# A two-layer graph kernel: front and edge steps re-ordered, a sum moved from POOL to PE, the bias added a step later

## The reference

```python
h = jnp.maximum(_layernorm(x, axis=-1), 0.0)
x = x + L0(h, adj)      # attention over the edges
h = jnp.maximum(_layernorm(x, axis=-1), 0.0)
x = x + L1(h, adj)      # hyperbolic midpoint over the edges

# L0
node_att = jax.nn.softmax(x @ node_w, axis=0)
h = x @ edge_w
e = jnp.where(adj > 0, h @ h.T, NEG_BIG)
edge_att = jax.nn.softmax(e, axis=1)
output = adj * (node_att * edge_att) @ (x @ weight) + bias

# L1: XW = mobius_matvec(W, X); gamma from the row lengths of XW
two_mean = (A @ (gamma * XW)) / clamp_abs(A @ (gamma - 1.0))
...         # two_mean scaled row by row, tanh and artanh of row lengths, relu
```

## Time and profile before

| | us |
|---|---|
| median of 3 runs (lowest, highest) | 722.23 (719.67, 728.56) |
| profiled execution | 725.74 |
| its span, first to last instruction | 724.0 |
| busy PE, DVE, POOL, ACT | 495.6, 471.4, 396.6, 350.2 |
| front, edge steps, second layer, last stage | 0 to 90, to 457, to 513, to 724 |

### The profile page before, as it was taken

One profiled execution on the slowest core, in us unless ns is written; L12 is line 12 of the kernel. 1 busy time (PEld: TensorE's weight loads), 2 busy tenths in 40 slices (PEclk: granted clock), 3 DMA queues, 4 the chain that ended last, 5 costly groups with the idle time before them and its releaser, 6 DMA issues.

```text
span 724.0 us, 12785 instructions
## 1 busy us (share of the span) xinstructions
PE 495.6 (68%) x3804; PEld 413.5 (57%) x3804; DVE 471.4 (65%) x1977; ACT 350.2 (48%) x718; POOL 396.6 (55%) x458
## 2 busy tenths in 40 slices
PE   3588463949698596988867877895266674757660
PEld 2367342738587485977766766784155553545440
DVE  3476757886877578686878578685444254476744
ACT  3596663655573555647340556477121121244553
POOL 4043537375655663566566610066477777777740
PEclk9798865959989899898989999998599798998885
DMA  8954579887879657786532400004433333335621
GB/s 310 394 204 173 189 283 366 291 314 254 291 232 369 219 219 266 244 342 211 185 94 67 101 17 1 1 1 148 147 97 99 103 100 97 97 106 159 193 75 59
DMA packets 38161, 128.92 MB, mean 178 GB/s; under 512 B 6224, under 2 KB 23504, under 8 KB 34000
## 3 DMA queue, kind: packets, MB, share of 16 engines
q1 hardware_dynamic: 22736, 84.87, 31.2%
q0 software_dynamic: 15360, 43.29, 21.3%
HBM read 115.49 MB, written 12.65 MB: 177 GB/s over the span
## 4 chain that ended last, share of the span: by engine, by line
PE 25%; DVE 25%; issue 13%; POOL 12%; ACT 9%; DMA 8%; DVEq 6%; ACTq 1%; POOLq 0%; SPq 0%
POOL work L1497 12%; PE bank L826 8%; DMA work<-in_adj 5%; PE bank L765 3%; ACT work L622 3%; DVE fs L1060 3%; PE bank L1589 2%; DVEq L1215 2%; PE bank L253 2%; PE bank L1768 2%; PE bank L797 2%; DMA table_h<-front 2%; DVE work L1104 1%; ACT L1211 1%; PE bank L810 1%
## 5 line engine op out<-in xcount | busy, mean ns | idle before, releaser
L720 POOL DMA_INDIRECT work<-table_h,work x160 | 161.4, 1009 | 99.6 <-issue 71.6
L1497 POOL DMA_INDIRECT work<-table_y,idx x128 | 130.7, 1021 | 39.0 <-issue 38.7
L622 ACT ACTIVATE work<-work 128x2048 bf16<-128x2048 f32 x64 | 121.6, 1902 | 45.6 <-DMA work<-in_adj 30.2
L826 PE MATMUL bank<-work 128*128 128x128 f32 x640 | 98.9, 318 | 15.7 <-DVEq L1106 15.7
L826 PEld LDWEIGHTS bank<-work 128*128 128x128 f32 x640 | 92.5, 230 | 17.5 <-DVEq L1106 15.0
L1589 PE MATMUL bank<-work 128*128 128x257 f32 x256 | 74.5, 442 | 19.8 <-DMA work<-table_y,idx 19.8
L765 PE MATMUL bank<-work 128*128 128x256 bf16 x512 | 70.8, 292 | 12.8 <-ACT work L622 12.8
L1589 PEld LDWEIGHTS bank<-work 128*128 128x128 f32 x256 | 55.4, 222 | 35.6 <-DMA work<-table_y,idx 26.4
L1585 PE MATMUL bank<-work 128*128 128x257 f32 x128 | 40.1, 440 | 48.9 <-ACT work L1600 40.5
L1362 DVE SCALAR_TENSOR_TENSOR fs<-work 128x256 f32<-128x256 f32 x32 | 13.7, 427 | 84.6 <-ACTq L1617 84.2
L765 PEld LDWEIGHTS bank<-work 128*128 128x128 bf16 x512 | 51.8, 104 | 27.3 <-ACT work L622 17.2
(11 more groups left out here) (271 smaller groups left out, 1006.6 us busy)
## 6 DMA issues: line engine op xcount, KB each, us to landing
work<-in_adj SPq DMA_DIRECT2D x32, 2048.0 KB, 9.7
table_y<-work SPq DMA_DIRECT2D x8, 520.0 KB, 3.7
gx<-in_x SPq DMA_DIRECT2D x8, 512.0 KB, 8.5
table_h<-front SPq DMA_DIRECT2D x8, 512.0 KB, 4.7
front<-in_x POOLq DMA_DIRECT2D x8, 512.0 KB, 5.0
out<-gx SPq DMA_DIRECT2D x8, 512.0 KB, 3.4
work<-table_h,work POOLq DMA_INDIRECT x160, 6.1
work<-table_y,idx POOLq DMA_INDIRECT x128, 2.8
```

The source lines that it names most:

```text
L622: a.activation(abf[:, u % HALVES, :], adu[:, b % 2, h, :], ACT.Copy, accum_out=cnt[:, k, b, h:h + 1]).then_inc(L["conv"], 1)
L720: p.indirect_dma_start(gat[:, k, n, :], None, table_h, bass.IndirectOffsetOnAxis(ix[:, k, n:n + 1], 0)) \
L826: last = t.matmul(bank[4 + b % 2][:, c * P:(c + 1) * P], gat[:, k, n, c * P:(c + 1) * P], otp[:, n, :], start=(q == 0), stop=(q == TILES - 1))
L1497: p.indirect_dma_start(gtm[:, n % OCT, q, :], None, table_y, bass.IndirectOffsetOnAxis(idx[:, n * TILES + q:n * TILES + q + 1], 0)) \
```

## The change

- SP: the sixth load of x and the store of group 0 come ahead of the second adjacency block, the weights and the bias behind all loads; blocks 2 to 5 are asked for after the stores of groups 1, 2, 4 and 6 (before: 1, 3, 5, 7).
- Front, beside the steps: units 3 to 7 are converted a step sooner and packed with them, `keys` run in steps 5 and 8 (before 6 and 9), the first list in step 9 (before 10), and four units of group 1 are converted in steps 9 and 10 (before two).
- Edge steps: ACT converts units 4 to 7 of group n and 0 to 3 of group n+1 (before 2 to 7 and 0, 1).
- Node softmax: the negation behind `edges`, the exponential behind the conversions, the sum over the partitions by a matmul with a matrix of ones, a step later.
- Bias: POOL adds it a step after the load, behind the next group's gathers.
- `spill_counts` in step 8, `spill_totals` amid POOL's gathers of step 8, `spill_places` in step 9, all 32 `spill_moves` on POOL behind the last aggregation.

```diff
+        STORED = (1, 2, 4, 6)
+        CONV_AT = (1, 2, 3, 3, 4, 5, 6, 7)
+        PACK_AT = (2, 3, 4, 4, 6, 6, 7, 8)
...
         def early_act(a):
             def beside(n):
-                if 1 <= n <= UNITS * GB:
-                    unit_conv(a, 0, 0, n - 1)
+                for u in range(UNITS * GB):
+                    if n == CONV_AT[u]:
+                        unit_conv(a, 0, 0, u)
+                if n == NG + 1:
+                    unit_conv(a, 1, 1, 0)
                 if n == NG + 2:
-                    unit_conv(a, 1, 1, 0)
-                    unit_conv(a, 1, 1, 1)
+                    for u in range(1, HALVES):
+                        unit_conv(a, 1, 1, u)
...
-                if ls and not at_:
-
-                    a.wait_ge(s_negmax, 1)
-                    a.activation(natt[:, :], logit[:, :], ACT.Exp, bias=cs(1)[:, 1:2], accum_out=cs(0)[:, 2:3])
-                    a.drain().then_inc(s_exp, 1)
...
-                for u in range(2, UNITS * GB):
+                for u in range(HALVES, UNITS * GB):
                     conv(u, wd)
+                conv(0, ahead)
+                conv(1, ahead)
+                if ls and not at_:
+                    a.wait_ge(s_negmax, 1)
+                    a.activation(natt[:, :], logit[:, :], ACT.Exp, bias=cs(1)[:, 1:2], accum_out=cs(0)[:, 2:3])
+                    a.drain().then_inc(s_exp, 1)
                 for b in (2, 3):
                     aggregate(b)
...
-                conv(0, ahead)
-                conv(1, ahead)
+                conv(2, ahead)
+                conv(3, ahead)
...
                         if n == GT // 2:
                             p.wait_ge(L["agg"], GB * g + GB)
                             p.sem_inc(s_go, 1)
+                            if isinstance(g, int) and g == NG - 1:
+                                spill_totals(p)
...
                     p.wait_ge(L["x1"], GB * g + GB)
-                    p.dma_start(xr2[:, k, :, :], x_r[:, grp(g), :]).then_inc(L["x"], 16)
-                    p.wait_ge(L["x"], 16 * (g + 1))
+                    p.dma_start(xr2[:, k, :, :], x_r[:, grp(g), :]).then_inc(L["x"][k], 16)
+                if at_:
+                    g, k = at_
+                    p.wait_ge(L["x"][k], 8 * (g - k) + 16)
                     for b in range(GB):
                         p.tensor_tensor(xr2[:, k, b, :], xr2[:, k, b, :], bias_bc[:, :], ALU.add)
                     p.drain().then_inc(L["xb"], 1)
...
                 exp_g(0, GT // 4)
+                if at_ and not ag_:
+                    t.wait_ge(s_exp, 1)
+                    t.matmul(exp_sum, ones, cs(0)[:, 2:3], start=True, stop=True).then_inc(s_sum, 1)
                 pack(2)
                 pack(3)
...
-                if n == 6:
+                if n == 5:
                     keys(d, 0, 0, 0, (6, 7))
+                if n == NG:
+                    keys(d, 0, 0, 1, (6, 7))
                 if n == NG + 1:
-                    keys(d, 0, 0, 1, (6, 7))
+                    edge_list(d, 0, 0, None)
                 if n == NG + 2:
                     d.drain()
                     d.tensor_reduce(cs(0)[:, 0:1], logit[:, :], AX, ALU.max)
                     d.drain().then_inc(s_red, 1)
-                    edge_list(d, 0, 0, None)
...
                 if ls:
                     edges(*ls)
-                if at_ and not ag_:
-                    d.wait_ge(s_all, 2)
-                    d.reciprocal(cs(1)[:, 3:4], cs(1)[:, 2:3])
...
+                if ls and not at_:
+                    d.wait_ge(s_all, 1)
+                    d.tensor_scalar(cs(1)[:, 1:2], cs(1)[:, 0:1], -1.0, None, ALU.mult)
+                    d.drain().then_inc(s_negmax, 1)
                 n = ag_[0] + 3 if ag_ and isinstance(ag_[0], int) else 0
+                if n == NG:
+                    spill_counts(d)
+                if n == NG + 1:
+                    spill_places(d)
...
-            norm_scale(d, f, 2)
-            if sparse:
-                spill_places(d)
...
-            if sparse:
-                spill_moves(d, range(0, 8))
...
             load(4)
+            load(5)
...
+            store(0, 0)
+            load_block(e, 1, 1)
+            load(6)
+            load(7)
             e.dma_start(w0[:, :, :], weight.rearrange("(c p) d -> p c d", p=P)).then_inc(s_w2, 16)
...
-            for g in range(NG):
+            for g in range(1, NG):
                 store(g, g % 2)
-                if g % 2:
-                    load_block(e, g // 2 + 2, g // 2 % 2)
+                if g in STORED:
+                    n = STORED.index(g) + 2
+                    load_block(e, n, n % 2)
...
-            p.wait_ge(s_exp, 1)
-            p.partition_all_reduce(cs(1)[:, 2:3], cs(0)[:, 2:3], P, RADD)
...
             fast_pool(p)
-            spill_totals(p)
             fast_flag(p)
             p.wait_ge(X["places"], 1)
-            spill_moves(p, range(16, NB))
-            p.drain().then_inc(X["move_pool"], 1)
+            p.wait_ge(L["agg"], GB * NG + 2 * GB)
+            spill_moves(p, range(NB))
+            p.drain().then_inc(X["move"], 1)
             table_pool(p, bf)
```

More of the change, by code:

```diff
@@ L581, in gnn_program @@
         L["adj"] = [sem(f"fa_adj{n}") for n in range(2)]
+        L["x"] = [sem(f"fa_xr{k}") for k in range(2)]
         L["gat"] = [[sem(f"fa_gat{k}{b}") for b in range(GB)] for k in range(2)]
@@ L773, in beside @@
             def beside(n):
-                if 2 <= n <= UNITS * GB + 1:
-                    unit_pack(t, 0, n - 2, (6, 7))
+                for u in range(UNITS * GB):
+                    if n == PACK_AT[u]:
+                        unit_pack(t, 0, u, (6, 7))
             return beside
@@ L1116, in body @@
                 if ls and not at_:
-                    d.wait_ge(s_all, 1)
-                    d.tensor_scalar(cs(1)[:, 1:2], cs(1)[:, 0:1], -1.0, None, ALU.mult)
-                    d.drain().then_inc(s_negmax, 1)
-                if ls and not at_:
                     for k in (0, 1):
@@ L1150, in body @@
                     dots(*at_, GT // 4, GT // 2)
+                if at_ and not ag_:
+                    d.wait_ge(s_sum, 1)
+                    d.reciprocal(cs(1)[:, 3:4], exp_sum)
+                    d.drain()
+                    d.tensor_scalar(natt[:, :], natt[:, :], cs(1)[:, 3:4], None, ALU.mult)
+                if at_:
                     by_slot(*at_)
@@ L1376, in gnn_program @@
         idb2, o = arena(o, P, dt=BF16)
+        move, _ = arena(o, NB, SW, dt=BF16)
         mm2, o = arena(o, 2, CW, dt=BF16)
@@ L1390, in gnn_program @@
         spill_idx, o = arena(o, OCT)
-        move, o = arena(o, NB, SW, dt=BF16)
+        assert o <= SPILL_END, o
         assert o <= WORK, o
@@ L1407, in gnn_program @@
         F["spill"] = [sem(f"fm_spill{k}") for k in range(2)]
-        X = {n: sem("sx_" + n) for n in ("counts", "total", "places", "move_dve", "move_pool", "found", "idx")}
+        X = {n: sem("sx_" + n) for n in ("counts", "total", "places", "move", "found", "idx")}
         def spill_counts(d):
@@ L1445, in spill_places @@
             d.tensor_scalar(part[:, 1, :].bitcast(I32), fifth, KEY - 1, None, ALU.bitwise_and)
-            d.drain().then_inc(X["places"], 1)
+            d.drain()
             for v in range(2):
                 d.tensor_copy(parts[:, :, v], part[:, v, :].bitcast(I32))
+            d.drain().then_inc(X["places"], 1)
         def spill_moves(v, blocks):
@@ L1455, in spill_pe @@
         def spill_pe(t):
-            t.wait_ge(X["move_dve"], 1)
-            t.wait_ge(X["move_pool"], 1)
+            t.wait_ge(X["move"], 1)
             for o in range(NB // OCT):
@@ L1865, in _ @@
             e.dma_start(bias_bc[:, :], bias.rearrange("(a d) -> a d", a=1).broadcast_to([P, D])).then_inc(s_w2, 16)
-            for g in range(5, NG):
-                load(g)
-            load_block(e, 1, 1)
-            def store(g, k):
-                e.wait_ge(f0.h, GB * (g + 1))
-                e.dma_start(th_r[:, grp(g), :], hs[:, k, :, :]).then_inc(s_th[k], 16)
-            for g in range(NG):
+            for g in range(1, NG):
                 store(g, g % 2)
-                if g % 2:
-                    load_block(e, g // 2 + 2, g // 2 % 2)
+                if g in STORED:
+                    n = STORED.index(g) + 2
+                    load_block(e, n, n % 2)
             fast_load(e)
```

19 lines of the change are left out of this document (9 added, 10 removed).

## The result

The changed kernel takes 744.5 us (median of 4; 741.9 to 748.4) beside 724.8 for the kernel before (4; 719.7 to 728.6). The ratio is 1.029, 95% interval 1.024 to 1.034: slower, and outside the predicted range. The profiled execution took 748.42 us, its span is 746.7; it is 3.9 us above its median, and the profile before 3.5 us above the 722.23 of the first three runs.

What follows compares the result with a forecast made beforehand. No engine was taken to bound the whole; DVE bound steps 3 to 7. Terms -8.7 + 0.4 + 0 + 0.3 + 17.9 + 1.0 - 1.4 = +9.5 us gave 735.2 profiled, median 732, range 715 to 742.

Steps and rivals of the forecast that it cites:

- The mechanism that it named first: POOL's configuration pairs around the totals' all-reduce in step 8 delay new_x of step 9: +17.9 us; forecast's case, chance 0.50.
- I take **0** for 3 and 4: Steps 3 to 7: sooner conversions and the later bias add together cost nothing; bounds -2.2 and +5 us.
- the sum has 0.3: Step 8: spill_counts adds one DVE instruction and a drain, +0.3 us.
- Part 1: Front: reordered transfers, earlier keys and first list bring PE's first list matmul sooner, -8.7 us; bounds -3 and -14.
- Part 2: Node softmax's maximum and sum: nothing themselves; second list -0.6 more, start of step 2 slower, together +0.4 us.
- Part 3: Sooner conversions, steps 3 to 7: at most 2.2 us of DVE's packing waits could return; taken as 0.
- Part 4: POOL adds the bias a step later; new_x keeps 0.2 us slack, cost 0, upper bound +5 us over five steps.
- the third rival: Late bias bounds steps 4 to 8, 2.7 us longer each, 13 us in all, 745 us; chance 0.10.
- Part 5: Totals amid step 8's gathers: new_x of step 9 late by +17.9 us; bounds +4.8 and +19.
- The clock term: After PE's long stand in step 9 its granted clock falls: +1 us, range 0 to 4.
- +4.8 (no time for either pair): Totals in step 8: lower bound of their cost if both POOL pairs take no time, +4.8 us.
- Part 6: Places hidden in step 9, 32 matrices on POOL with 8.9 us to spare; first steps and second layer gain, -1.4 us.

Runs made afterwards that it cites:

- experiment 8: Kernel before with only the front's changes (load and store order, earlier conversions and packing, earlier keys and first list): 724.2 us beside 723.1, ratio 1.003.
- experiment 11: Changed kernel with the bias in its own step, totals by a PE matmul and ScalarE's conversions as before: 715.6 us, ratio 0.986 to the kernel before.
- experiment 9: Kernel before with the node softmax's changes alone, ratio 0.987, and with the front's changes too, 0.984, on a chip where the kernel before took 892.3 us.
- experiment 10: Changed kernel with the bias in its own step and totals by a PE matmul, run twice: 717.2 and 714.7 us, ratios 0.993 and 0.987 to the kernel before.
- experiment 5: Kernel before with the late bias alone, added behind the next group's gathers: 735.7 us beside 723.1, ratio 1.019.
- experiment 4: Changed kernel with the totals by a PE matmul instead of POOL's all-reduce, late bias kept: 729.1 us, ratio 1.011 to the kernel before.
- experiment 1: Changed kernel with the totals behind the last bias add and the places in step 10, late bias kept: 735.5 us, ratio 1.020 to the kernel before.
- experiment 2: Changed kernel with the bias added in its own step, totals still amid the gathers of step 8: 719.6 us, ratio 0.995 to the kernel before.
- experiment 6: Changed kernel with the bias add moved ahead of the next group's gathers, totals still amid step 8's gathers: 719.7 us, ratio 0.993 to the kernel before.
- experiment 3: Changed kernel with the bias in its own step, totals behind the last bias add and places in step 10: 721.4 us, ratio 0.998 to the kernel before.
- experiment 7: Changed kernel with one small POOL operation added in step 1: a copy, 744.9 us, ratio 1.031; then a tensor_tensor, 742.2 us, ratio 1.023 to the kernel before.

## Why the prediction was wrong

The forecast was 732 and its range ended at 742; it came to 744.5. The mechanism that it named first was there in full; what failed was the step "I take **0** for 3 and 4".

The profiled executions were to lie 9.5 us apart and lie 22.7 apart. Of the 13.2 us between, 8.8 came in steps 3 to 8, where the sum has 0.3 and the trace 9.1 (5.1, 1.2 and 2.8); there `new_x` waited 8.1 us for `xb`. The second list is 1.5 us behind its forecast, step 2 has 1.9 us more than it was given, step 9 has 2.0 more, the second layer 1.4 less, and the last stage 0.4 more.

*Part 1, the front.* -7.5 instead of -8.7, and L226 without a wait for the store. Right for the front, but not for what follows: alone it is worth nothing (experiment 8). Of the maximum and the exponential the text says that `edges` and the conversions no longer stand behind them, and it books that at nothing. It is this edit that moved the second list (experiment 11 against 8), and by experiment 9 perhaps without help from the front.

*Part 2.* The second list came at 112.6 (111.2 forecast). The all-reduce came at 95.8 instead of 91.7, as its pair took 9.8 us and not 6.3, and DVE's negation stood 3.4 us for it. Then step 2 lost 2.9 us where 1.0 stood: from the second list to its end 39.4 us, before 36.5. It is the conversions of group 2 ahead of the copies for PE, as the step had it, under-sized: with them as before (experiment 11) it is 36.4, with bias and totals alone undone (experiment 10) 39.5.

*Part 3, conversions,* 0, and measured the same (experiment 11): what they cost in step 2 comes back by the end, and no more.

*Part 4, the late bias.* Forecast 0, bounds -2.2 and +5; measured 12.6 us alone (experiment 5), 12.0 us with the totals on PE (729.1 against 717.2), and 25 us beside the totals on POOL (744.5 against 719.6). The drain of 4.61 us was the right row for the adds, and the releases in the loop came 5.1 to 5.5 us behind their start, half a microsecond more: `new_x` of steps 4, 6 and 7 waited 0.6 to 0.8 us for it, as the bound had it. What I left out is where the gathers end. I looked at the steady state, one step of 41.8 us, and there POOL is ahead. In steps 8 and 9 a step has no new group to find and is 34 us long, while POOL's twenty gathers and their wait for PE keep their length. There the adds start behind the last gather, at 412 to 414 in experiments 4 and 1, and `new_x` at 417 to 419.5 instead of 415. It could be read from the earlier trace rows: the load of x is issued at 413.36 for 0.80 us, and with 4.61 us for adds and drain the bias is there at 418.8, 3.8 us behind the 414.96. It is the mechanism of the third rival, for the most part in steps 8 and 9 rather than in each of steps 4 to 8; that rival's price, 13 us, is met by chance, and so is its 745 by the 744.5.

*Part 5, the totals.* Nearly exact, in part by luck. Of the shift of `new_x` in step 9, 414.96 to 437.33, 4.2 us were brought along from step 8; the other 18.2 stand against 17.9. The pairs took 5.7 and 7.8 us (6.3 and 8.0 forecast), the load of x is 7.3 us later by this part (6.5 forecast), and `new_x` starts 3.8 us behind the adds (4.6 forecast): the last two cancel. The clock term was 1 and is 2.7 us: from `new_x` to the end of step 9 it took 25.1 us, before 22.4, at a clock of 0.58 in the first ten. But "+4.8 (no time for either pair)" was wrong in kind. In size it is not what the part's own terms give, 17.9 - 6.3 - 8.0 = 3.6; without pairs, `new_x` measured from the end of step 8 came 4.3 us later (15.7 against 11.4), and all of that is the late bias. The totals cost 1 to 5 us while the bias is early (experiments 2 and 6 against 10) and 15 us while it is late (744.5 against 729.1): the second pair is on the way only if the adds come behind the all-reduce. The two parts are not a sum: each makes the other costlier, and I had put the whole of it on one of them.

*Part 6.* The places were hidden in step 9, as forecast; uncovered they cost some 5 us (24.2 against 19.3 us for step 10, experiment 3). The matrices took 29.69 us and were ready 7 us before POOL was wanted (8.9 forecast). The second layer, last `new_x` to the first gather of the last stage, went from 57.1 to 54.3 us, -2.8 instead of -1.4.

```profile
480.11 29.69 POOL L1480 TENSOR_SCALAR work<-work 128x256 bf16<-128x256 f16 x32 [33.00 <-PE bank L843]
509.97 0.20 POOL L1735 MEMSET work<- 128x128 f32 x1 [0.17 <-issue]
516.76 4.00 POOL L1724 TENSOR_SCALAR work<-work,col 128x256 f32<-128x256 f32 x4 [6.58 <-DVEq L1835]
```

The step of the first pair, 11.65 us ahead of the first add in step 2, has no term in the sum. Before the change it stood in step 1 and delayed the gathers of step 2 instead. Of the 5.1 us of step 3 it makes at most 4 (experiment 7); the rest of them is open, since the versions with a late bias and the pair in that place take from 41.3 us (experiment 5) to 46.9 for step 3. The changed kernel and the versions of experiments 1 and 4 have the same instructions up to step 8, and step 3 took 46.9, 44.4 and 43.1 us in them; with the bias in its own step it took 41.1 to 42.0.

## What to carry to other kernels

Work moved to another place of a queue is priced in the shortest steps too, at the end of the pipeline where it empties, and not in the steady state alone: there the moved work still has its full length and the others have lost theirs. Two edits that meet in one queue are costed together; here they make 13 and 1 to 5 us alone and 27 in company. And a gain ahead of a wait is only a gain once one has seen what else that wait stands for: behind the front it was an all-reduce, and the edit that took the engines out of its way was booked at nothing.

## What the runs showed of the hardware

*The pair belongs to the kind of operation.* Ahead of the first all-reduce behind tensor operations and ahead of the first tensor_tensor or tensor_scalar behind an all-reduce there is a pair of MODIFY_POOL_CONFIG; a copy (122.75, and the CAST at 446.93 behind the flag's all-reduce) and the gathers run without one.

*It takes longer beside transfers.* From the pair to the all-reduce: 5.7 us at 1 GB/s (404.5 to 410.2), 6.3 at 260 in the kernel before (85.6 to 91.9), 9.8 at 396 (86.0 to 95.8). To the tensor_tensor: 7.8 us at 79 GB/s (425.8 to 433.6), 11.5 at 254 (151.4 to 162.9). But for the tensor_tensor the rate alone does not give the time: in the kernel before it took 8.0 us at 273 GB/s (127.7 to 135.7). Here are 9.8, 11.5 and 8.0, with the columns of the stretches above:

```profile
86.00:95.80 9.80, 4.39 (x40) 2.65 (x38) 6.28 (x20) 5.62 (x6) 0.00 (x0) 0.67 0.95 396
151.40:162.90 11.50, 9.56 (x82) 9.08 (x80) 7.73 (x26) 6.61 (x17) 0.00 (x0) 0.67 0.72 254
127.70:135.70 8.00, 8.00 (x64) 6.70 (x62) 5.66 (x29) 6.47 (x8) 0.04 (x1) 0.84 0.81 273
```

The Trainium skill, "GPSIMD Engine Reference", section 2.1 Instruction dispatch, gives approximately 6 µs for such a load. The quiet all-reduce agrees with 5.7; the measured times beside transfers, up to 11.5 us, and the 7.8 us of the tensor_tensor decide where the page is lower. That the transfers are the cause was not tested by itself.

*A stand costs more than its length.* In step 9 the dot products wait for `new_x`. Where PE stood some 19 us for them, its granted clock in the ten microseconds that followed `new_x` was 0.58 (the changed kernel, and 0.64 and 0.58 in the two forms of experiment 7); where it stood 4.8 to 5.1 us (experiments 1, 4 and 5), 0.66, so that it was at the level of 1.2 GHz for a part of them; where it stood 0.5 us, in the kernel before, 1.00. From `new_x` to the end of the step it took 24.4 to 25.2 us behind a stand of either length, 22.4 before. That the clock is the cause of this was not tested by itself. The ten microseconds behind the stand of experiment 1:

```profile
419.50:429.50 10.00, 7.33 (x42) 5.33 (x42) 7.84 (x39) 8.36 (x17) 3.32 (x5) 0.66 0.00 1
```
